# A decoder's wide cross-attention: where the key and query projections stand in TensorE's round

## The chip, the cores and the metric

The kernel runs on one core of a Trainium2 chip. The core has TensorE (matmuls), VectorE, ScalarE, GpSimd and SyncE, which work from queues of their own and wait for each other on semaphores. The metric is the device time of one execution in microseconds; the time of the kernel before is the median of three runs, 3679.55 us.

## The reference

Two decoder layers on x of 1024 x 128, each with self-attention, cross-attention to a context of 6404 x 96, and a small mixture of experts. The change lies in the last cross-attention, with 16 heads of 64:

```
q = query @ w_q                      # 1024 x 1024, from x of 1024 x 128
k, v = split(context @ w_kv)         # 6404 x 1024 each
scores = einsum('bhqd,bhkd->bhqk', q, k) * 64 ** -0.5
attn = softmax(scores)
out = einsum('bhqk,bhkd->bhqd', attn, v)
x = x + out @ w_out + b_out
```

Everything is computed in fp32 accuracy: q and k are each split into a rounded part (hi) and a rest (lo), and scores are hi x hi + hi x lo + lo x hi.

## The kernel before

`wide_heads_and_experts` (from line 1947) computes this attention. The heads are taken in 8 pairs, the 1024 queries in 2 halves of 512, which makes 16 units. A unit goes through the 6404 keys in 51 steps of 128 keys. Two steps make a round, so there are 408 rounds. The two heads of a pair stand side by side in the array.

In each round TensorE does, in the order in which its block is written (the loop behind line 2469):

- `score` of two steps (L2432): 12 matmuls, three products for each of two heads and two steps, into four PSUM banks. ScalarE takes exp of each step (L2595) into a ring of six buffers.
- `early`: one pair of maximum matmuls (L2387), bf16, two heads at once, for the *next* unit: they give rough scores from which VectorE takes the maximum of each row (L2668, two reductions), which is subtracted later ahead of exp.
- `weigh` of the two steps before (L2458): the value products, four pairs of fp32 matmuls that accumulate in bank 4.
- `whole`: at most one other piece of work (below).
- `late`: the remaining maximum pairs of the round, mostly one.

The pieces in `whole` are called items: "k" (L2405) projects 512 keys (the last chunk of 13 has 260) of the next pair of heads, "q" (L2398) projects the 512 queries of the unit after the next, "t" (L2393) turns the maxima, "s" (L2410) adds up the sums of the exponentials, and "y" (L2416) is the output projection. A planner at the head of the function hands them out: a "k" item in every sixth step (91 in the loop, 8 in an even unit and 5 in an odd one), one "q" item per unit until unit 13 (14), and one of each of the others per unit.

All items and the maximum pairs share a ring of three PSUM banks (`SIDE`, `BANKS` = 3). A maximum pair takes the next two banks, an item the next one; each waits (`wait_place`) until what stood in its bank three places earlier has been read. For a "k" item ScalarE first copies the result (L2556, `att_k_raw`), after the two exponentials of the round; then VectorE subtracts that copy from the result in PSUM (L2686, `att_k_step`), which frees the bank. In the next round ScalarE rounds (L2576, L2580), and in the one after that GpSimd makes the rest (L2264). For "q" ScalarE makes two copies (L2552, L2553) and VectorE subtracts (L2677). Each engine goes through the items in the order early, whole, late. VectorE's queue is therefore: reductions of the early pair, in some rounds a piece of a reciprocal (L2701), the subtraction of the item, reductions of the late pairs.

GpSimd adds the exponentials of half of the steps into a total (L2305) and issues DMAs that add the others (L2294). SyncE loads the values in groups of four steps.

Of the kernel before, what the change touches and what calls it, by code (L numbers as in the profile page):

```python
# [1946 lines left out]
def wide_heads_and_experts(nc, name, net_name, PS, ident, ctxT, xn, xnT, x, O, A, values, out, wide):  # L1947
# [61 lines left out]
    tiled, whole, taken, turned = [], [], PER_UNIT, 1  # L2009
    for j in range(STEPS):  # L2010
# [9 lines left out]
        items = whole[-1]  # L2020
# [11 lines left out]
            items.append(("k", p + 1, f))  # L2032
    last_items = [("s", UNITS - 1), ("y", UNITS - 1)]

    early = [items[:1] for items in tiled]
    late = [items[1:] for items in tiled]
    order = first + [item for items in zip(early, whole, late) for part in items for item in part] + last_items
# [13 lines left out]
    def top_later(item):  # L2051
        return item[1] > 0 and item[2] < KF - 1
# [78 lines left out]
    def bank_of(item, s=0):  # L2131
        return first_bank[item] + s if item in first_bank else SIDE + (place[item] + s) % BANKS
# [4 lines left out]
    def strip(s):  # L2137
        return slice(s * DH2, (s + 1) * DH2)

    def chunk(f):  # L2140
        return slice(f * HALF, min(NCTX, (f + 1) * HALF))
# [4 lines left out]
    with ExitStack() as stack:  # L2146
# [204 lines left out]
        def _(pe):  # L2351
            def wait_first(item):

                if item in copy_number:
                    pe.wait_ge(tile_copied, copy_number[item] + 1)
                elif item is not None:
                    pe.wait_ge(dve_freed, dve_count[item + (1,) if item[0] == "m" else item])

            def wait_place(at):
                if at < BANKS:  # L2360
                    wait_first(ring_user[at])
                else:
                    who, count = freed[at - BANKS]
                    pe.wait_ge(dve_freed if who == "dve" else negated, count)

            def side(item):
                kind, n = item[0], item[1]
                alone = item in first_bank
                if alone:
                    wait_first(first_user[item])  # L2370
                else:
                    wait_place(place[item])
                if kind == "m":
                    if not alone:
                        wait_place(place[item] + 1)
                    c, qt = item[2:]
                    p = n // HALVES
                    w = min(HALF, NCTX - c * HALF)
                    if qt == 0:
                        if c == 0:  # L2380
                            pe.wait_ge(kept, hi_count[("q", n)])
                        if n % HALVES == 0 and not top_later(("k", p, c)):
                            pe.wait_ge(kept, hi_count[("k", p, c)])
                        if n % HALVES == 0 and top_later(("k", p, c)):
                            pe.wait_ge(topped, top_number[("k", p, c)])
                    for s in range(2):
                        ins = pe.matmul(PS[:, bank_of(item, s), 0:w], q_top[strip(s), n % 2, qt * P:(qt + 1) * P],  # L2387
                                        k_top[strip(s), c * HALF:c * HALF + w], start=True, stop=True,
                                        tile_position=(s * DH2, 0))
                elif kind == "t":  # L2390
                    pe.wait_ge(top_ready, 2 * (n + 1))
                    for qt in range(QT):
                        ins = pe.transpose(PS[:, bank_of(item), qt * P:(qt + 1) * P], top[:, qt, :], ident[:, :])  # L2393
                elif kind == "q":
                    p, hf = n // HALVES, n % HALVES
                    if hf == 0:
                        pe.wait_ge(in_loaded[p % 2], 32 * (p // 2 + 1))
                    ins = pe.matmul(PS[:, bank_of(item), :], wq[:, p % 2, :], xnT[:, hf * HALF:(hf + 1) * HALF],  # L2398
                                    start=True, stop=True)
                elif kind == "k":  # L2400
                    p, f = n, item[2]
                    if f == 0:
                        pe.wait_ge(in_loaded[p % 2], 32 * (p // 2 + 1))
                    c = chunk(f)
                    ins = pe.matmul(PS[:, bank_of(item), 0:c.stop - c.start], wk[:, p % 2, :], ctxT[0:DC, c],  # L2405
                                    start=True, stop=True)
                elif kind == "s":
                    pe.wait_ge(folded, n + 1)
                    for s in range(2):
                        ins = pe.matmul(PS[strip(s), bank_of(item), :], ones_wide[:, :], total[:, n % 2, s, :],  # L2410
                                        start=True, stop=True, tile_position=(0, s * DH2))
                else:
                    pe.wait_ge(scaled, n + 1)
                    pe.wait_ge(out_loaded[n // HALVES % 2], 16 * (n // HALVES // 2 + 1))
                    for qt in range(QT):
                        ins = pe.matmul(PS[:, bank_of(item), qt * D:(qt + 1) * D], out_u[:, qt * P:(qt + 1) * P],  # L2416
                                        wo[:, n // HALVES % 2, :], start=True, stop=True)
                ins.then_inc(side_filled, 1)

            def score(j):  # L2420
                n, kt = j // KT, j % KT
                p, hf, b = n // HALVES, n % HALVES, 2 * (j % 2)
                if j >= 2:
                    pe.wait_ge(exped, j - 1)
                if kt == 0:
                    pe.wait_ge(dve_freed, dve_count[("q", n)])
                if kt % 4 == 0 and hf == 0:
                    pe.wait_ge(lo_left, lo_number[("k", p, kt // 4)])
                keys = slice(kt * P, (kt + 1) * P)
                for k, q, last in ((k_hi, q_hi, False), (k_hi, q_lo, False), (k_lo, q_hi, kt >= 2)):  # L2430
                    for s in range(2):
                        i = pe.matmul(PS[:, b + s, :], k[p % 2][strip(s), keys], q[n % QBUFS][strip(s), :],  # L2432
                                      start=kt < 2 and k is k_hi and q is q_hi, stop=last,
                                      tile_position=(s * DH2, 0), skip_group_check=kt >= 2)
                if kt >= 2:
                    i.then_inc(scored, 1)

            def subtract_maxima(j):

                n, kt, b = j // KT, j % KT, 2 * (j % 2)  # L2440
                if kt == 0:
                    pe.wait_ge(negated, negated_count[("t", n)])
                for s in range(2):
                    r = 32 * (b + s)
                    i = pe.matmul(PS[:, b + s, :], key_ones[r:r + 32, :], minus_max[r:r + 32, :],
                                  start=False, stop=True, tile_position=(r, 0))
                i.then_inc(scored, 1)
# [21 lines left out]
            for j in range(0, STEPS, 2):  # L2469
                score(j)  # L2470
                if j % KT == 1:
                    subtract_maxima(j)
                score(j + 1)
                if j % KT == 0:
                    subtract_maxima(j)
                if (j + 1) % KT < 2:
                    subtract_maxima(j + 1)
                for item in early[j // 2]:
                    side(item)
                between = j >= 2 and (j - 1) % KT == 0  # L2480
                if j >= 2:
                    weigh(j - 2)

                    if between:
                        assert not whole[j // 2]
                        for item in late[j // 2]:
                            side(item)
                    weigh(j - 1)
                for item in whole[j // 2] + ([] if between else late[j // 2]):
                    side(item)  # L2490
                if j // KT == LAST:
                    if j % KT == NET["turn"]:

                        pe.wait_ge(dve_freed, dve_count[("y", LAST - 1)])
                        pe.wait_ge(negated, negated_count[("s", LAST - 1)])
                        net.turn_tokens(pe, net.glue(0), 0)
                    if j % KT == NET["score"]:
                        net.score(pe, 0)
                    if j % KT == NET["turn_gates"]:
                        net.turn_gates(pe, 0)  # L2500
                    if j % KT == NET["spread"]:
                        net.spread_gates(pe, 0, 0)
# [560 lines left out]
```

## Time and profile before

| | |
|---|---|
| median of 3 runs | 3679.55 us (3679.04 to 3690.73) |
| the profiled execution | 3683.04 us |
| its span (first to last instruction) | 3681.3 us |
| TensorE matmuls busy | 3390.7 us, 92% |
| VectorE, ScalarE, GpSimd busy | 69%, 62%, 62% |
| first score of the wide attention | 1683.7 us after the span's start |

"Busy" is the time in which at least one instruction of an engine is under way. Matmuls overlap and their ends are modelled, so the distance from one start to the next says more than the duration of one. In a timeline, the time in brackets is the idle time of the engine just before the row, with what ended it. Rows with a count (x2, x4) are several instructions of one form merged, with the time from the first's start to the last's end.

### The profile page before, as it was taken

What the parts mean: (1) busy time and instruction counts of PE and PEld (TensorE: products, weight loads), DVE (VectorE), ACT (ScalarE), POOL (GpSimd) and SP (SyncE); (2) the same over time, 40 slices, a digit from 0 to 9 for tenths busy, and PEclk for the clock granted to TensorE, in tenths of its full rate; (3) what the DMA queues carried; (4) which work ended last, traced back from release to release, by engine and by line L of the source; (5) the groups of instructions that cost most, each with busy time, mean ns of one, the idle gap of its engine ahead of it and who ended that gap; (6) DMA issues with size and microseconds to landing.
All of it is one profiled execution on the core that took longest, in us unless ns stands there. A gap on an engine that the chain in (4) does not pass through costs nothing.

```text
span 3681.3 us, 58339 instructions
## 1 busy us (share of the span) xinstructions
PE 3390.7 (92%) x21696; PEld 1320.1 (36%) x21696; DVE 2537.5 (69%) x4290; ACT 2283.1 (62%) x2759; POOL 2268.9 (62%) x1564
## 2 busy tenths in 40 slices
PE   5877999999999989988999999999999999999999
PEld 2331222222222224433444444444444444444444
DVE  5748888888888835766666666666666666665842
ACT  4657888888888873575555555555555555555422
POOL 3124565665656600305888888888888888888800
PEclk7968999999999999978999999999999999999999
DMA  4111002002000100343566666676666766678100
GB/s 138 55 34 21 1 2 37 2 1 37 1 2 1 54 1 5 145 159 77 123 139 147 131 137 128 141 148 131 134 130 143 143 133 134 132 166 192 29 0 6
DMA packets 123729, 307.46 MB, mean 84 GB/s; under 512 B 15395, under 2 KB 31861, under 8 KB 122773
## 3 DMA queue, kind: packets, MB, share of 16 engines
q0 software_dynamic: 49680, 180.90, 24.7%
q1 hardware_dynamic: 73772, 122.82, 12.2%
q8 instruction: 179, 2.93, 0.3%
q14 instruction: 98, 0.80, 0.1%
HBM read 88.15 MB, written 34.64 MB: 33 GB/s over the span
## 4 chain that ended last, share of the span: by engine, by line
PE 47%; DVE 5%; ACT 2%; issue 1%; POOL 0%; DVEq 0%; ACTq 0%
PE PS L2458 20%; PE PS L2432 12%; PE PS L2387 6%; PE PS L2405 3%; DVE att_top_piece L2668 2%; PE PS L340 2%; PE PS L348 1%; DVE att_k_step L2686 1%; PE PS L341 1%; ACT att_k_raw L2556 1%; PE PS L2398 1%; PE PS L2416 0%; DVE k_xn L2725 0%; PE PS L2410 0%; ACT att_prob L2547 0%
## 5 line engine op out<-in xcount | busy, mean ns | idle before, releaser
L2668 DVE TENSOR_REDUCE att_top_piece<-PS 128x1 f32<-128x512 f32 (+1 forms) x1560 | 968.9, 665 | 346.0 <-PE PS L2387 343.4
L2305 POOL TENSOR_TENSOR att_total<-att_total,att_prob 128x1024 f32<-128x1024 f32 (+1 forms) x417 | 1053.5, 2526 | 152.2 <-ACT att_prob L2595 143.7
L2595 ACT ACTIVATE att_prob<-PS 128x1024 f32<-128x1024 f32 x816 | 792.6, 1021 | 562.7 <-PE PS L2432 501.3
L1781 ACT ACTIVATE att_prob<-PS 128x1024 f32<-128x1024 f32 (+2 forms) x912 | 892.3, 1004 | 178.5 <-PE PS L1623 175.7
L1878 DVE TENSOR_REDUCE att_top_piece<-PS 128x1 f32<-128x512 f32 (+1 forms) x1459 | 905.3, 665 | 131.9 <-PE PS L1591 126.7
L2458 PE MATMUL PS<-att_prob,att_vals 128*64 128x512 f32 x3264 | 794.5, 607 | 5.7 <-issue 4.9
L1646 PE MATMUL PS<-att_prob,cross_Vst 128*32 128x256 f32 (+1 forms) x5544 | 506.7, 431 | 2.1 <-issue 0.2
L1493 POOL TENSOR_TENSOR att_stage<-att_stage,att_run 128x512 f32<-128x512 f32 x150 | 191.1, 1274 | 401.6 <-ACT att_stage L1760 401.3
L1591 PE MATMUL PS<-cross_Kstack,cross_Qmax 49*128 49x512 bf16 (+1 forms) x1664 | 323.4, 386 | 95.5 <-DVE att_top_piece L1878 33.5
L2432 PE MATMUL PS<-att_q_hi,att_k_hi 64*128 64x512 f32 x1632 | 395.2, 480 | 4.2 <-POOL att_k_lo L2264 2.6
L2387 PE MATMUL PS<-att_k_top,att_q_top 64*128 64x512 bf16 (+1 forms) x1664 | 325.3, 389 | 76.1 <-DVE att_top_piece L2668 66.8
L2432 PE MATMUL PS<-att_q_hi,att_k_lo 64*128 64x512 f32 x1632 | 323.8, 393 | 0.0
L2432 PE MATMUL PS<-att_q_lo,att_k_hi 64*128 64x512 f32 x1632 | 322.3, 391 | 0.0
L1623 PE MATMUL PS<-cross_Qscore,cross_Kstack 49*128 49x512 bf16 x1632 | 308.6, 380 | 10.6 <-ACT att_prob L1781 6.3
L2458 PEld LDWEIGHTS PS<-att_prob,att_vals 128*64 128x64 f32 x3264 | 198.0, 136 | 332.1 <-issue 244.5
L1591 PEld LDWEIGHTS PS<-cross_Kstack,cross_Qmax 49*128 49x128 bf16 x1664 | 100.5, 93 | 490.0 <-DVE att_top_piece L1878 340.2
L2387 PEld LDWEIGHTS PS<-att_k_top,att_q_top 64*128 64x128 bf16 x1664 | 84.3, 93 | 510.3 <-DVE att_top_piece L2668 288.0
L1495 POOL TENSOR_SCALAR att_stage<-att_stage 128x512 f32<-128x512 f32 x150 | 222.8, 1486 | 13.1
L1646 PEld LDWEIGHTS PS<-att_prob,cross_Vst 128*32 128x32 f32 x5544 | 110.4, 108 | 275.5 <-ACT att_prob L1781 189.2
L1497 POOL TENSOR_TENSOR att_run<-att_run,att_stage 128x512 f32<-128x512 f32 x150 | 190.8, 1272 | 12.5
L2264 POOL TENSOR_TENSOR att_k_lo<-att_k_step,att_k_hi 128x512 fp32r<-128x512 f32 (+1 forms) x104 | 152.9, 1480 | 73.3 <-ACT att_k_hi L2580 73.1
L2686 DVE TENSOR_TENSOR att_k_step<-PS,att_k_raw 128x512 f32<-128x512 f32 (+2 forms) x104 | 67.6, 650 | 180.7 <-ACT att_k_raw L2556 163.8
(328 smaller groups left out, 3684.2 us busy)
## 6 DMA issues: line engine op xcount, KB each, us to landing
k_O<-att_prob POOLq DMA_DIRECT2D x180, 512.0 KB
k_xn<-att_prob POOLq DMA_DIRECT2D x165, 512.0 KB, 5.3
att_vals<-values SPq DMA_DIRECT2D x192, 256.0 KB, 3.0
values<-att_prob SPq DMA_DIRECT2D x14, 1024.0 KB, 4.1
values<-cross_Vall SPq DMA_DIRECT2D x10, 1024.0 KB, 4.2
cross_Kstack<-kparts SPq DMA_DIRECT2D x36, 204.0 KB
f_w<-in_f_w SPq DMA_DIRECT2D x24, 256.0 KB, 4.5
kparts<-cross_Vst SPq DMA_DIRECT2D x24, 128.0 KB, 1.8
```

Source lines behind the costliest of these rows:

```text
L1495: pool.tensor_scalar(now, now, 0.0, None, ALU.max).then_inc(tile_ahead, 1)
L1591: i = pe.matmul(PS[:, banks[item][s], 0:w], Qm[rows, g % 2, a, at:at + P], Kst[rows, g % 2, a, c * HALF:c * HALF + w], start=True, stop=Tr ...
L1623: i = pe.matmul(PS[:, 2 * (e % 2) + s, lo:HALF], Kst[rows, g % 2, a, kt * P:(kt + 1) * P], Qs[rows, g % 2, a, n % HALVES * HALF + lo:(n % ...
L1646: ins = pe.matmul(PS[r:r + 32, PV, lo:queries.stop], Vst[:, u % 2, kt, s, :], prob[:, j % RING, par, s, lo:queries.stop], start=(i == 0), ...
L1781: act.activation(prob[:, j % RING, par, :, lo:HALF], PS[:, 2 * (e % 2):2 * (e % 2) + 2, lo:HALF], ACT.Exp, scale=scale).then_inc(exped, 1)
L1878: dve.tensor_reduce(top_piece[:, n % 2, s * QT + qt, c:c + 1], PS[:, banks[item][s], 0:w], AX, ALU.max).then_inc(dve_freed, 1)
L2305: pool.tensor_tensor(so_far, so_far, prob[0:rows, j % RING, :, :], ALU.add).then_inc(summed, 1)
L2387: ins = pe.matmul(PS[:, bank_of(item, s), 0:w], q_top[strip(s), n % 2, qt * P:(qt + 1) * P], k_top[strip(s), c * HALF:c * HALF + w], start ...
L2432: i = pe.matmul(PS[:, b + s, :], k[p % 2][strip(s), keys], q[n % QBUFS][strip(s), :], start=kt < 2 and k is k_hi and q is q_hi, stop=last, ...
L2458: i = pe.matmul(PS[strip(s), PV, :], vals[:, value_slot(n, kt // 4), kt % 4, strip(s)], prob[:, j % RING, s, :], start=(kt == 0), stop=(kt ...
L2595: act.activation(prob[:, j % RING, :, :].rearrange("p a b -> p (a b)"), PSf[:, b:b + 2 * HALF], ACT.Exp, scale=scale).then_inc(exped, 1)
L2668: dve.tensor_reduce(top_piece[:, n % 2, s * QT + qt, c:c + 1], PS[:, bank_of(item, s), 0:w], AX, ALU.max).then_inc(dve_freed, 1)
```

## The change

In the planner each round's `whole` list is sorted so that "q" and "k" items come first. In TensorE's loop these items are issued between the early maximum pair and the value products; all other items stay behind the products. The blocks of the other engines are not touched.

```diff
@@ -2032,6 +2032,8 @@
             items.append(("k", p + 1, f))
     last_items = [("s", UNITS - 1), ("y", UNITS - 1)]
 
+    for items in whole:
+        items.sort(key=lambda item: item[0] not in ("q", "k"))
     early = [items[:1] for items in tiled]
     late = [items[1:] for items in tiled]
     order = first + [item for items in zip(early, whole, late) for part in items for item in part] + last_items
@@ -2478,6 +2480,9 @@
                 for item in early[j // 2]:
                     side(item)
                 between = j >= 2 and (j - 1) % KT == 0
+                projected = [item for item in whole[j // 2] if item[0] in ("q", "k")]
+                for item in projected:
+                    side(item)
                 if j >= 2:
                     weigh(j - 2)
 
@@ -2486,7 +2491,7 @@
                         for item in late[j // 2]:
                             side(item)
                     weigh(j - 1)
-                for item in whole[j // 2] + ([] if between else late[j // 2]):
+                for item in whole[j // 2][len(projected):] + ([] if between else late[j // 2]):
                     side(item)
                 if j // KT == LAST:
                     if j % KT == NET["turn"]:
```

## Rows read from the trace of the kernel before

**Rows 1.** The page, chain that ended last, share of the span by line.
```profile
PE PS L2458 20%; PE PS L2432 12%; PE PS L2387 6%; PE PS L2405 3%; DVE att_top_piece L2668 2%; PE PS L340 2%; PE PS L348 1%; DVE att_k_step L2686 1%; PE PS L341 1%; ACT att_k_raw L2556 1%; PE PS L2398 1%; PE PS L2416 0%; DVE k_xn L2725 0%; PE PS L2410 0%; ACT att_prob L2547 0%
```

**Rows 2.** Windows: stretch and length, then busy us of PE, PEld, DVE, ACT, POOL; clock.
```profile
2500.00:3290.00 790.00, 759.50 (x4504) 335.65 (x4502) 512.84 (x832) 431.78 (x515) 670.34 (x414) 1.00 0.66 138
```

**Rows 3.** Waits from 1800 to 3300: waiter, awaited, total us, times, longest.
```profile
POOL att_total L2305 <- ACT att_prob L2595: 110.1, 86, 2.8
...
PE PS L2387 <- DVE att_top_piece L2668: 56.0, 104, 1.2
```

**Rows 4.** Timeline of TensorE, a projection round and two plain rounds: start us, us, what.
```profile
2396.48 0.58 PE L2432 MATMUL PS<-att_q_hi,att_k_hi 64*128 64x512 f32 x2
...
2400.25 1.13 PE L2405 MATMUL PS<-k_ctxT,k_wk 96*128 96x512 f32 x2
2401.31 0.39 PE L2387 MATMUL PS<-att_k_top,att_q_top 64*128 64x512 bf16 x2
2401.35 0.58 PE L2432 MATMUL PS<-att_q_hi,att_k_hi 64*128 64x512 f32 x2
...
2403.48 0.39 PE L2387 MATMUL PS<-att_k_top,att_q_top 64*128 64x512 bf16 x2 [0.39 <-DVE att_top_piece L2668]
...
2405.71 0.58 PE L2432 MATMUL PS<-att_q_hi,att_k_hi 64*128 64x512 f32 x2
...
2407.06 0.40 PE L2432 MATMUL PS<-att_q_hi,att_k_lo 64*128 64x512 f32 x2
2407.30 0.39 PE L2387 MATMUL PS<-att_k_top,att_q_top 64*128 64x512 bf16 x2
2407.61 1.94 PE L2458 MATMUL PS<-att_prob,att_vals 128*64 128x512 f32 x8
2409.49 0.39 PE L2387 MATMUL PS<-att_k_top,att_q_top 64*128 64x512 bf16 x2
2409.52 0.58 PE L2432 MATMUL PS<-att_q_hi,att_k_hi 64*128 64x512 f32 x2
```

**Rows 5.** Timelines of VectorE and of ScalarE in the same rounds.
```profile
2402.05 0.69 DVE L2686 TENSOR_TENSOR att_k_step<-PS,att_k_raw 128x512 f32<-128x512 f32 x1 [2.26 <-ACT att_k_raw L2556]
2402.65 2.55 DVE L2668 TENSOR_REDUCE att_top_piece<-PS 128x1 f32<-128x512 f32 x4
...
2406.10 1.29 DVE L2668 TENSOR_REDUCE att_top_piece<-PS 128x1 f32<-128x512 f32 x2
2407.73 1.29 DVE L2668 TENSOR_REDUCE att_top_piece<-PS 128x1 f32<-128x512 f32 x2 [0.33 <-PE PS L2387]
...
2412.75 0.94 DVE L2701 RECIPROCAL att_sums<-att_sums 128x128 f32<-128x128 f32 x1
...
2401.42 0.60 ACT L2556 ACTIVATE att_k_raw<-PS 128x512 f32<-128x512 f32 x1 [1.90 <-PE PS L2405]
...
2406.80 1.94 ACT L2595 ACTIVATE att_prob<-PS 128x1024 f32<-128x1024 f32 x2 [1.24 <-PE PS L2432]
```

**Rows 6.** Timelines of TensorE, VectorE, ScalarE behind a query projection's round.
```profile
1966.86 0.58 PE L2432 MATMUL PS<-att_q_hi,att_k_hi 64*128 64x512 f32 x2
...
1972.77 0.58 PE L2432 MATMUL PS<-att_q_hi,att_k_hi 64*128 64x512 f32 x2
...
1968.05 0.69 DVE L2677 TENSOR_TENSOR att_q_lo<-PS,att_q_hi 128x512 fp32r<-128x512 f32 x1 [1.89 <-ACT att_q_top L2553]
...
1967.42 0.59 ACT L2553 ACTIVATE att_q_top<-PS 128x512 bf16<-128x512 f32 x1
```

**Rows 7.** Timeline of TensorE behind a short key projection's round.
```profile
2104.26 0.40 PE L2432 MATMUL PS<-att_q_hi,att_k_lo 64*128 64x512 f32 x2
2104.60 0.39 PE L2387 MATMUL PS<-att_k_top,att_q_top 64*128 64x512 bf16 x2
```

**Rows 8.** Timeline of TensorE, a projection round with two late pairs.
```profile
1704.44 0.58 PE L2432 MATMUL PS<-att_q_hi,att_k_hi 64*128 64x512 f32 x2
...
1711.44 0.39 PE L2387 MATMUL PS<-att_k_top,att_q_top 64*128 64x512 bf16 x2 [1.78 <-DVE att_top_piece L2668]
```

## The prediction

> **What bounds the kernel now.** I read the chain that ended last first: TensorE lines carry most of it, and VectorE's maximum (L2668) and key subtraction (L2686) appear in it for 2% and 1% of the span [rows 1]. So TensorE is the bound, and something on VectorE gets onto its path in places. The windows by stage come next: in a stretch of the wide attention, TensorE is busy 759.50 of 790.00 us at a granted clock of 1.00, which is its upper level, 2.4 GHz; VectorE has 512.84 and GpSimd 670.34 [rows 2]. At most 4% is there to win in this stage, if nobody works faster. The waits say where it is: in 1500 us TensorE waited 56.0 us for VectorE's maximum, 104 times, and GpSimd waited for the exponentials (110.1 us on one line alone), so it keeps up [rows 3]. The same list names only TensorE as what ScalarE's exponentials wait for, never GpSimd or a DMA.
>
> The timeline shows which rounds wait. Take the first score of a round as time 0. A plain round (2405.71 to 2409.52) lasts 3.81 us: early pair at 1.59, value products from 1.90, late pair at 3.78 [rows 4]. The round with a key projection (2396.48 to 2401.35) lasts 4.87; the projection stands at 3.77 and the late pair at 4.83 [rows 4]. The round behind it is as plain as the other, yet lasts 4.36 (2401.35 to 2405.71), because its early pair goes at 2.13 and not at 1.59 [rows 4]: 0.54 lost. Its cause can be read off the other engines. The projection comes out at the round's end, 1.17 us after its issue ScalarE copies it (2401.42, 0.60), VectorE, which has nothing else it may do, stands idle 2.26 us until that copy and subtracts (2402.05, 0.69), and only then reduces the late pair (from 2402.65) [rows 5]. In the plain round those reductions begin at 0.39 and end at 1.68 (2406.10 plus 1.29) [rows 5]; here they begin at 1.30. The early pair needs the bank of the first of them and goes 0.14 us after it ends.
>
> **The change part by part.** No instruction is added or taken away. The 91 key and 14 query projections of the loop (no round holds two) go ahead of the four value products, and the two products' waits, the exponentials of the previous round, are long met. The sort does nothing: each round of the planner's list holds at most one item of the kind it sorts. The order in which the results are counted (early, whole, late) and the ring of three banks stay as they were, so ScalarE, VectorE and GpSimd keep their order, and no queue of SP is passed. What moves is the start of each projection, from 3.77 to about 1.90, and of its round's products, from 1.90 to 2.96 (1.06 is the distance from projection to late pair, 2400.25 to 2401.31) [rows 4].
>
> New timetable of a projection round: early pair 1.59; projection 1.90; products 2.96; late pair 2.96 + 1.88 (2407.61 to 2409.49) = 4.84; end 4.87, as before [rows 4]. ScalarE ends its two exponentials at 3.03 (2406.80 plus 1.94) [rows 5] and the result is there at 1.90 + 1.17 = 3.07, so the copy runs to 3.67 and the subtraction from 3.70 to 4.39. VectorE has finished the early reductions at 3.31 (2407.73 plus 1.29); in rounds with a piece of the reciprocal (0.94) it is free at 4.25 and ends the subtraction at 4.94 [rows 5]. The late pair reaches VectorE only 0.43 us after its issue (2407.30 to 2407.73) [rows 4, 5], at 5.27. So the subtraction fits into a gap, the late reductions start at 0.40 of the next round, as in a plain one, and that round's early pair goes at 1.59. The stall behind a key projection goes whole; what is late next is TensorE's own stream, 3.81 us.
>
> A query projection has two copies and then its subtraction. Now the latter starts at 1968.05, 1.19 into the round (1966.86), and the round behind it, which holds a key projection too, lasts 5.91 (1966.86 to 1972.77) and not 4.87: 1.04 lost [rows 6]. Afterwards: the second copy ended at 1968.01 (1967.42 plus 0.59) [rows 6], 1.15 after the round's start, where a key's copy begins at 0.07 (2401.42) [rows 5], so about 1.08 for both; 3.07 + 1.08 = 4.15, subtraction to 4.87, or 4.94 behind a reciprocal, still ahead of 5.27. This stall goes as well.
>
> The waits the projection itself has: its bank is the third of the ring, last held by the second half of the previous round's late pair, whose reduction ends at 1.68 [rows 5]. With the 0.14 of a release that is 1.82, and TensorE comes there at 1.90: no wait, by 0.08 us. Behind a round with a reciprocal the reductions end at most 0.1 later. Queued behind this wait are now the products; nobody waits for these soon (the exponentials reuse their buffer six steps on, values are loaded three groups ahead).
>
> The trace has no projection between a maximum pair and a product, so its borders are priced from both sides. The pair of score matmuls takes 0.24 (2407.06 to 2407.30), the early pair before products 0.31: a border of about 0.08 [rows 4]. Products to late pair are 1.88, where four of 0.43 (1.94 us for all four with their tail) would be 1.72: 0.16. A new border may cost 0.16 more or less than the one it replaces: 105 x 0.16 = 17 us either way. I take 0, because a projection has two borders in either place and its cost between products and late pair, 1.06, already holds both kinds. The Trainium skill, "TensorEngine Tiling (Array Packing)", Key Properties, says that a change of the tiling mode drains TensorE. By that rule the sum stays: pair, projection, products, pair are three changes of mode, as are pair, products, projection, pair. No run here shows the drain apart.
>
> The sum. Of the 91 key projections 7 are short (260 columns). Behind a short one the early pair stands 0.34 behind the last score (2104.26 to 2104.60), against 0.24: 0.1 x 7 = 0.7 [rows 7]. Two of the 84 long ones stand in rounds with two late pairs. There the second late pair waits for reductions that are behind the subtraction: it goes at 7.00 (1704.44 to 1711.44) [rows 8]. Afterwards it goes at 5.27 + 0.65 + 0.14 = 6.06: 0.94 x 2 = 1.9. The other 82 are followed by a round that loses 0.55: 45.1. Queries: 14 x 1.04 = 14.6. Together 0.7 + 1.9 + 45.1 + 14.6 = 62.3 us. The profiled execution took 3683.0 (span 3681.3 and 1.7 around it), 3.5 above the median of the runs. From its time the sum gives 3620.7, from the median of 3679.6 it gives 3617.
>
> **The rivals.**
> A, the stall is given back in part: the margin of 0.08 us is not there, because the projection's bank is freed a little later or the release takes longer at this place, or the borders cost more. For: 0.08 is less than one release of 0.14. Against: the plain rounds repeat to 0.01 us, and a release that is due before TensorE arrives costs nothing. At 0.3 us for each of 105 projections 31 us come back: 3648.
> B, nothing: what is removed on TensorE is at once taken by the next, GpSimd. Its 670.34 us of 790 [rows 2] would have to fit into some 760: 88%. It waits for ScalarE now [rows 3], so I hold that for unlikely; in that case 3679.
> C, slower: the projection waits for reductions of its own round. Place: the wait for its bank, ahead of the products. If the bank were one of the early pair's, free at 3.31 + 0.14 = 3.45 [rows 5], TensorE would stand 1.55 us in each of 105 rounds: 163 - 62 = 101 more, 3780. It decides from a wait of 62.3 / 105 = 0.6 us, a bank free later than 2.4 instead of 1.68. Against: the ring's arithmetic (pair 2 banks, projection the third).
> D, the change doesn't do what it says: the subtraction is not what holds the early pair. Then the round lengths stay, 3679. Against: idle time and release agree in each of the rounds read [rows 4, 5, 6].
>
> **How the numbers follow.** The forecast, all stalls gone, with the border's bounds: 3617, 3600 to 3634, chance 0.76. A 0.13 (3634 to 3660), B and D 0.05 (3668 to 3690), C 0.06. The likeliest case gives 3617. For 8 in 10 I take the lower bound a little in, 3603, and reach into A up to 3648. About 0.3% (11 us) is what a measurement of this kernel can tell from no change; all of the forecast and of A lie beyond it: faster 0.89, same 0.05, slower 0.06.
>
> **What would show it.** In the profile afterwards: rounds with a projection stay at 4.87, the ones behind them fall to 3.81, a key round behind a query round from 5.91 to 4.87. TensorE's wait for L2668 ahead of L2387 falls from 56 us in 1500 to under 20, what is left standing at the units' beginnings. VectorE's idle time ahead of L2686 stays of the order of 0.4 us each. Wrong would be: a new wait at the projections (L2405, L2398) on L2668 (A, C), value products dearer behind a projection (A), exponentials waiting for GpSimd (B), or unchanged 4.36 us rounds (D).

## The result and the profile after

The changed kernel takes 3617.58 us (median of 4 runs, 3616.33 to 3618.99). The kernel before, with one more run on the same chip, has a median of 3682.96 us (3679.04 to 3690.73). The ratio is 0.9832, with a 95% interval of 0.9814 to 0.9849. The forecast was 3617, reckoned from the first three runs' median of 3679.6: 62 us less. Measured by the four runs, it is 65 us less.

The profiled execution spans 3617.3 us, 64.0 less than that of the kernel before. The window of the wide attention, to be laid beside [rows 2] (columns as there):

```profile
2500.00:3200.00 700.00, 691.68 (x4140) 307.63 (x4140) 477.95 (x765) 398.23 (x477) 616.92 (x381) 1.00 0.68 142
```

TensorE is busy for 98.8% of this stretch, not 96.1%, at the same granted clock, its upper level of 2.4 GHz. GpSimd is at 88%, as the text of rival B had worked out, and still waits for ScalarE. The list of waits from 1800 to 3300 us has these rows, beside [rows 3]:

```profile
POOL att_total L2307 <- ACT att_prob L2600: 82.2, 75, 1.8
...
DVE att_k_step L2691 <- ACT att_k_raw L2561: 23.3, 57, 0.5
PEld PS L2407 <- DVE att_top_piece L2673: 16.5, 70, 0.3
PE PS L2389 <- DVE att_top_piece L2673: 15.2, 15, 1.2
```

TensorE's wait ahead of the maximum pairs is down from 56.0 us in 104 places to 15.2 us in 15 places. Seven of these are at the start of an even unit, where the prediction expected what is left, but the other eight are at the end of one. VectorE's subtraction waits 0.4 us each time (23.3 / 57). The projection's weight loads name VectorE 70 times, but its matmuls have no such row: they start 0.32 us behind the early pair, except in one kind of round (below).

The same three rounds as in [rows 4], TensorE:

```profile
2366.36 0.58 PE L2434 MATMUL PS<-att_q_hi,att_k_hi 64*128 64x512 f32 x2
...
2367.94 0.39 PE L2389 MATMUL PS<-att_k_top,att_q_top 64*128 64x512 bf16 x2
2368.26 1.12 PE L2407 MATMUL PS<-k_ctxT,k_wk 96*128 96x512 f32 x2
2369.32 1.94 PE L2460 MATMUL PS<-att_prob,att_vals 128*64 128x512 f32 x8
2371.19 0.39 PE L2389 MATMUL PS<-att_k_top,att_q_top 64*128 64x512 bf16 x2
2371.23 0.58 PE L2434 MATMUL PS<-att_q_hi,att_k_hi 64*128 64x512 f32 x2
...
2372.81 0.39 PE L2389 MATMUL PS<-att_k_top,att_q_top 64*128 64x512 bf16 x2
...
2375.04 0.58 PE L2434 MATMUL PS<-att_q_hi,att_k_hi 64*128 64x512 f32 x2
```

The projection round lasts 4.87 us (2366.36 to 2371.23), as before. The round behind it lasts 3.81 (to 2375.04) and not 4.36, and its early pair goes at 1.58 and not at 2.13. VectorE and ScalarE in the same rounds, beside [rows 5]:

```profile
2368.38 1.29 DVE L2673 TENSOR_REDUCE att_top_piece<-PS 128x1 f32<-128x512 f32 x2 [0.34 <-PE PS L2389]
2370.06 0.69 DVE L2691 TENSOR_TENSOR att_k_step<-PS,att_k_raw 128x512 f32<-128x512 f32 x1 [0.39 <-ACT att_k_raw L2561]
2371.62 1.29 DVE L2673 TENSOR_REDUCE att_top_piece<-PS 128x1 f32<-128x512 f32 x2 [0.87 <-PE PS L2389]
...
2367.45 1.94 ACT L2600 ACTIVATE att_prob<-PS 128x1024 f32<-128x1024 f32 x2 [0.41 <-PE PS L2434]
2369.43 0.60 ACT L2561 ACTIVATE att_k_raw<-PS 128x512 f32<-128x512 f32 x1
```

The copy follows the exponentials without a gap. The subtraction runs from 3.70 to 4.39 of its round, and the late reductions start at 5.26 (2371.62), when their own matmuls come out. What names VectorE's idle time ahead of them is now TensorE: in these rounds the order on VectorE costs nothing any more.

### The profile page after: what moved, and what is told of

Same layout as the page of the kernel before. It is cut to its first block, busy times and chain, and to the rows that moved or that the text cites. A ratio compares the mean times of both kernels' runs of the same rounds, so it can differ in the third digit from the quotient of the medians.

```text
span 3617.3 us, 58339 instructions
## 1 busy us (share of the span) xinstructions
PE 3369.8 (93%) x21696; PEld 1316.2 (36%) x21696; DVE 2548.1 (70%) x4290; ACT 2283.4 (63%) x2759; POOL 2269.3 (63%) x1564
## 4 chain that ended last, share of the span: by engine, by line
PE 52%; DVE 2%; issue 1%; ACT 1%; POOL 0%; DVEq 0%; ACTq 0%
PE PS L2460 21%; PE PS L2434 16%; PE PS L2389 6%; PE PS L2407 3%; PE PS L340 2%; PE PS L348 2%; PE PS L341 1%; PE PS L2400 1%; PE PS L2418 0%; DVE att_top_piece L2673 0%; DVE k_xn L2730 0%; ACT att_prob L2552 0%; PE PS L2412 0%; PE PS L2447 0%; PE PS L2395 0%
## 5 line engine op out<-in xcount | busy, mean ns | idle before, releaser
L2307 POOL TENSOR_TENSOR att_total<-att_total,att_prob 128x1024 f32<-128x1024 f32 (+1 forms) x417 | 1070.5, 2567 | 116.7 <-ACT att_prob L2600 108.4
L2296 POOL DMA_DIRECT2D k_O<-att_prob x165 | 163.2, 989 | 51.2 <-ACT att_prob L2600 48.0
```

The source lines that it names most:

```text
L2307: pool.tensor_tensor(so_far, so_far, prob[0:rows, j % RING, :, :], ALU.add).then_inc(summed, 1)
```

## The experiments

The theory is that of the prediction: a projection's subtraction stands ahead of the late reductions in VectorE's queue, and it waits for ScalarE's copy of a result that comes at the round's end. The rivals are that the gain belongs to the round as a whole, that it is in proportion to how much earlier the projection goes, or that it comes from the projection's own bank. "Loop" below is the time from the first score of the first round to the first score of the last one: 1806.8 us in the kernel before, 1748.5 in the changed one.

**One kind of projection alone.**

```diff
-                projected = [item for item in whole[j // 2] if item[0] in ("q", "k")]
+                projected = [item for item in whole[j // 2] if item[0] == "k"]
```

> The change for the key projections alone; the 14 query projections stay behind the products. Theory (VectorE's queue: the subtraction waits for ScalarE's copy and holds up the late reductions, each stall of its own): the 1.04 us behind each query round stay, 14 x 1.04 = 14.6 us of the 62.3 are not won, so about 3632 us, rounds behind a key 3.81, rounds behind a query 4.85 (plain) and 5.91 (key). Rival (the gain comes from the round as a whole, for example products that start later): the query rounds make no difference of their own beyond their share of the count, 14 of 105, so 8 us: 3626.

Measured: 3631.44 us (3626.0 to 3635.82), ratio 0.9863 (0.9848 to 0.9878). And with `== "q"`:

> The change for the 14 query projections alone. Theory: 14.6 us are won, 3680 - 15 = 3665; rounds behind a key stay at 4.36, rounds behind a query fall to 3.81 and 4.87. Rival (share by count): 8 us, 3672.

Measured: 3663.38 us (3661.43 to 3670.6), ratio 0.9954 (0.9939 to 0.9969). Both medians are within 2 us of what the theory gives, and 5 and 9 us from the rival. For the first run that decides nothing, since its single times reach down to the rival's 3626. The rounds decide: in the second run those behind a query last 3.81 and 4.86 us, those behind a key 4.36. The 14 rounds behind a query are 14.6 us shorter in all than before. The whole loop is only 11.3 shorter (1795.5), because in three of its first six rounds, which the edit doesn't touch, the lower granted clock cost 3.3 us more than it did in the kernel before. In the first run there is one surprise. The key round behind a query round lasts 6.09 us and not 5.91:

```profile
2169.77 0.39 PE L2389 MATMUL PS<-att_k_top,att_q_top 64*128 64x512 bf16 x2 [0.88 <-DVE att_top_piece L2673]
2170.27 1.13 PE L2407 MATMUL PS<-k_ctxT,k_wk 96*128 96x512 f32 x2
```

The projection goes 0.50 behind the early pair and not 0.32. The previous round's late reductions were held up by the query's subtraction, so the projection's bank came free late, with the products queued behind it. This is the mechanism of rivals A and C, 0.18 us in 7 rounds. The query part of the change takes it away.

**How much later may it go.** The projection between the two steps' products:

```diff
-                for item in projected:
-                    side(item)
                 if j >= 2:
                     weigh(j - 2)
+                for item in projected:
+                    side(item)
+                if j >= 2:
```

> The projection between the two steps' value products, some 0.9 us later than in the change. Theory: issue 2.80, result 3.97, key copy to 4.57, subtraction to 5.29, late reductions from 5.29 in place of 5.27: nothing lost for keys. Queries: copies to 5.05, subtraction to 5.77, the first late reduction ends at 6.42 and the next early pair can go at 1.69 in place of 1.59: 0.1 x 14 = 1.4 us. So about 3619. Rival (the gain is in proportion to how much earlier the projection goes: 1.87 us earlier gave 62): 0.97 us earlier gives 32, 3648.

Measured: 3637.42 us (3632.69 to 3642.6), ratio 0.9881 (0.9864 to 0.9898), loop 1764.9. Neither number. As the theory says, the stall is gone: rounds behind a key last 3.81, and behind a query 3.84. But each projection round lasts 5.02 and not 4.87. TensorE:

```profile
2377.12 1.08 PE L2460 MATMUL PS<-att_prob,att_vals 128*64 128x512 f32 x4
2378.13 1.12 PE L2407 MATMUL PS<-k_ctxT,k_wk 96*128 96x512 f32 x2
2379.18 1.08 PE L2460 MATMUL PS<-att_prob,att_vals 128*64 128x512 f32 x4
2380.19 0.39 PE L2389 MATMUL PS<-att_k_top,att_q_top 64*128 64x512 bf16 x2
```

Half of the products takes 1.01 us (2377.12 to 2378.13 and 2379.18 to 2380.19), so two halves take 2.02, where the whole takes 1.87 (2369.32 to 2371.19 in the changed kernel). 0.15 x 105 = 15.8 us, and the loop is 16.4 longer than in the changed kernel. The expectation had left out that this place adds a border: the products are cut in two.

**The other way round.** The projection goes behind the late pair, on TensorE and on VectorE, later than in the kernel before. Two new helpers split a list: `projections` gives its "q" and "k" items, `others` the rest.

```diff
...
-    order = first + [item for items in zip(early, whole, late) for part in items for item in part] + last_items
+    order = first + [item for e, w, l in zip(early, whole, late) for item in e + others(w) + l + projections(w)
+                     ] + last_items
...
-                for item in whole[j // 2] + ([] if between else late[j // 2]):
+                for item in others(whole[j // 2]) + ([] if between else late[j // 2]) + projections(whole[j // 2]):
...
-                for item in whole[j // 2] + late[j // 2]:
+                for item in others(whole[j // 2]) + late[j // 2] + projections(whole[j // 2]):
```

> The other way round: on TensorE and on VectorE the projection goes behind the late maximum pair, so it comes out even later than before the change, but nothing stands behind its subtraction in that round. Theory (what costs is only that the late reductions stand behind the subtraction on VectorE): late reductions run at 4.21 to 5.50, the subtraction at 5.89 to 6.58, which is 1.02 to 1.71 of the next round, ahead of its early reductions at 2.02; the stalls go as with the change, about 3617 (3612 to 3622). Rival (the projection has to come out earlier, because its own bank or its copy is what the early pair waits for, or because the products must cover the copy): the early pair waits as before or longer, 3680 or more.

Measured: 3638.97 us (3634.68 to 3644.77), ratio 0.9885 (0.987 to 0.9901), loop 1766.7. The kernel is 1.1% faster than before although every projection comes out later, and the rival's 3680 is refuted: the early pair doesn't need an early projection. One thing this run can't tell. In the order early, whole, late the next early pair takes the projection's bank and that of the first late reduction; in the turned order it takes the late pair's banks alone. So the run removes a possible wait for the projection's own bank too. That this wait wasn't the one that counted is read from the kernel before: the subtraction ended at 2402.74 (2402.05 plus 0.69), 0.74 us ahead of the early pair at 2403.48, and the first late reduction at 2403.34 (2402.65 plus the 0.69 that one takes), 0.14 ahead [rows 4, 5].

VectorE in a projection round and behind it:

```profile
2379.72 1.29 DVE L2675 TENSOR_REDUCE att_top_piece<-PS 128x1 f32<-128x512 f32 x2 [0.34 <-PE PS L2394]
2381.91 1.29 DVE L2675 TENSOR_REDUCE att_top_piece<-PS 128x1 f32<-128x512 f32 x2 [0.90 <-PE PS L2394]
2383.59 0.69 DVE L2693 TENSOR_TENSOR att_k_step<-PS,att_k_raw 128x512 f32<-128x512 f32 x1 [0.39 <-ACT att_k_raw L2563]
2384.78 1.29 DVE L2675 TENSOR_REDUCE att_top_piece<-PS 128x1 f32<-128x512 f32 x2 [0.50 <-PE PS L2394]
```

The late reductions come first (2381.91) and the subtraction fits ahead of the next early ones. What was won less than expected is again a border:

```profile
2381.48 0.39 PE L2394 MATMUL PS<-att_k_top,att_q_top 64*128 64x512 bf16 x2
2381.80 1.13 PE L2412 MATMUL PS<-k_ctxT,k_wk 96*128 96x512 f32 x2
2382.86 0.51 PE L2439 MATMUL PS<-att_q_hi,att_k_hi 64*128 64x512 f32 x2
...
2386.54 0.39 PE L2394 MATMUL PS<-att_k_top,att_q_top 64*128 64x512 bf16 x2
```

From late pair to late pair, one round on, it is 5.06 us (2381.48 to 2386.54). Projection and plain round together last 8.87, against 8.68 in the changed kernel: 0.19 for each of 105 projections, 20 us, where the loop is 18.2 longer (1.4 of the difference is a round of the changed kernel that a fall of the clock lengthened, below). Late pair and scores, which otherwise follow each other without a border, are parted here.

**The copy twice.** ScalarE copies each key projection twice.

```diff
+        copied_once, copied_twice = m.sem("copied_once"), []
...
+                    copied_twice.append(item)
+                    act.activation(k_raw[n % 2][:, to], PS[:, bank_of(item), 0:to.stop - to.start], ACT.Copy
+                                   ).then_inc(copied_once, 1)
+                    act.wait_ge(copied_once, len(copied_twice))
                     raw = act.activation(k_raw[n % 2][:, to], PS[:, bank_of(item), 0:to.stop - to.start], ACT.Copy)
```

> The kernel before with the same second copy. Theory: each second copy behind the products lengthens the wait of the next early pair by its whole duration: 84 x 0.63 for long keys and 7 x 0.4 for short ones, 56 us, and up to 8 before the loop: 3736 to 3744; rounds behind a key 4.99. Rival (the stall has another cause, the copy is covered): 3680 to 3688.

In the kernel before: 3742.1 us (3739.47 to 3743.15), ratio 1.0175 (1.016 to 1.019), loop 1865.6, 58.8 longer. Rounds behind a key last 4.99. Of the 58.8, 54.2 us are in the rounds behind a key and the two key rounds with two late pairs. The rest lies almost all in three other rounds, in each of which the granted clock fell to its lower level (near 1713, 1775 and 1819 us).

> The changed kernel with ScalarE's copy of each key projection (L2556 of before) done twice, one after the other; the result is the same. Theory: the subtraction ends at 4.39 + 0.63 = 5.02, still ahead of the late pair at 5.27, so the 91 copies of the loop cost nothing. The 13 before the loop may cost up to 13 x 0.6 = 8: 3617 to 3625. Rival (the copy is still on the path of the round): 91 x 0.6 = 55 more, 3672.

In the changed kernel: 3625.89 us (3616.01 to 3633.49), ratio 0.9859 (0.9835 to 0.9883), loop 1748.7, that is 0.2 us longer. The same addition costs 54 us in one place and nothing in the other. The whole kernel is 9.5 us slower than the changed kernel in the runs beside it (3616.42, below). The expectation allowed 8 for the 13 copies ahead of the loop. How much of the 9.5 is theirs stays open, because what lies ahead of the loop differs by more than that from trace to trace ("Luck in the last figure", below). The subtraction in each, VectorE, first in the kernel before with the second copy, then in the changed one:

```profile
2430.41 0.69 DVE L2691 TENSOR_TENSOR att_k_step<-PS,att_k_raw 128x512 f32<-128x512 f32 x1 [2.89 <-ACT att_k_raw L2561]
2431.01 2.54 DVE L2673 TENSOR_REDUCE att_top_piece<-PS 128x1 f32<-128x512 f32 x4
```

```profile
2376.33 0.69 DVE L2696 TENSOR_TENSOR att_k_step<-PS,att_k_raw 128x512 f32<-128x512 f32 x1 [1.02 <-ACT att_k_raw L2566]
2377.27 1.29 DVE L2678 TENSOR_REDUCE att_top_piece<-PS 128x1 f32<-128x512 f32 x2 [0.25 <-PE PS L2390]
```

VectorE's idle time ahead of the subtraction grows by 0.63 in both (2.26 to 2.89, 0.39 to 1.02). In the second it comes out of the wait ahead of the late reductions, which still has 0.25 left.

**What the rest is made of.** The 15 waits left are in rounds with two late pairs (one round has three), whose second needs a bank that the first one's reduction frees. This run moves all but the last late pair of such rounds between the products:

```diff
+                split = j >= 2 and not between and len(late[j // 2]) > 1 and len(projected) == len(whole[j // 2])
...
+                    elif split:
+                        for item in late[j // 2][:-1]:
+                            side(item)
                     weigh(j - 1)
-                for item in whole[j // 2][len(projected):] + ([] if between else late[j // 2]):
+                for item in whole[j // 2][len(projected):] + ([] if between else late[j // 2][-1:] if split
+                                                              else late[j // 2]):
```

> The changed kernel, and in rounds with two or more late pairs all but the last go between the two steps' products. Those rounds last 5.09 to 6.14 where the stream would need some 0.25 more than a plain round. Theory: the second late pair waits for the first one's reduction, so pulling the first one forward by about 0.9 us wins up to 0.9 in each of some 12 such rounds (7 at the end of even units, 5 in the first unit); the 7 at the start of even units win nothing, because the copy of the output stands ahead of the reductions on VectorE. 5 to 10 us less than the changed kernel: 3607 to 3612. Rival (VectorE's total work in such rounds is the bound): no difference, 3617.

Measured: 3611.72 us (3609.6 to 3615.64), ratio 0.9823 (0.9808 to 0.9838). The changed kernel beside it, on the same chip:

> The changed kernel once more, beside the others on the same chip: 3617 us, and the loop from its first to its last round some 58 us shorter than before. What the part ahead of the loop takes, which the change does not touch, should then agree with the kernel before to within the few us that the moments of TensorE's clock changes differ by.

Measured: 3616.42 us (3614.22 to 3625.89), ratio 0.9839 (0.9824 to 0.9855), loop 1746.3. The two medians differ by 4.7 us and the intervals overlap, so the times alone leave the rival open; the split version's loop is 1742.6. The rounds at the end of even units fall from 5.59 to 4.80, as expected. Those at the start are not neutral, though. They rise from 5.88 to 6.35:

```profile
2342.22 0.39 PE L2389 MATMUL PS<-att_k_top,att_q_top 64*128 64x512 bf16 x2
2342.54 1.08 PE L2460 MATMUL PS<-att_prob,att_vals 128*64 128x512 f32 x4
2345.10 0.39 PE L2389 MATMUL PS<-att_k_top,att_q_top 64*128 64x512 bf16 x2 [1.48 <-DVE att_top_piece L2678]
```

```profile
2343.67 0.69 DVE L2717 COPY att_out_u<-PS 128x512 f32<-128x512 f32 x1 [1.06 <-PE PS L2460]
2344.27 1.95 DVE L2678 TENSOR_REDUCE att_top_piece<-PS 128x1 f32<-128x512 f32 x3
```

There the copy of the output (L2717 of this run) stands ahead of the late reductions on VectorE and waits for the unit's last product. With the pair between the products, that product ends later, and so do copy and reductions. The next run leaves these rounds alone (`split = j >= 2 and j % KT and ...`):

> As the run that split the late pairs, but not in the rounds at the start of an even unit, which its trace shows lengthened from 5.88 to 6.36 us; the others keep what they won there (5.60 to 4.80 at the end of the 7 even units, 0.6 to 0.8 in five rounds of the first unit). Theory: 7 x 0.48 = 3.4 us less than that run and about 9 less than the changed kernel: 3608 (3605 to 3612). Rival (what is won at a unit's end is given back at the start of the next, whatever stands there): no better than that run, 3612.

Measured: 3609.38 us (3603.84 to 3613.02), ratio 0.9806 (0.9786 to 0.9827), loop 1736.6.

> The changed kernel beside it on the same chip: 3617 us, ratio to before 0.983 to 0.984; no two theories are told apart, it is the measure for the other run of this call.

Measured: 3616.94 us (3612.57 to 3622.43), ratio 0.983 (0.981 to 0.985), loop 1748.2. The last version is 7.6 us ahead of the changed kernel by the medians, but the two intervals against the kernel before overlap. In the traces the gain is plain: the loop is 11.6 us shorter, 9.2 of them in the 12 rounds that the split touches and the rest where the clock falls differ. The rounds at the start of even units are back at 5.88 while those at their end stay at 4.80. It is the best version seen.

## Why the prediction was right

**The cause.** The step that mattered is that VectorE "has nothing else it may do": a queue in order, in which the subtraction stands ahead of the late reductions. Four kinds of experiment bear it out: the order on the queues is turned round and the stall goes, though every projection comes out later (projection behind the late pair, with the trace's reading of the banks); only the copy is lengthened and the stall grows by just that, or not at all; each kind of projection gives its own share; and half of the advance in time gives the whole of the stall.

**The timetable.** Projection 1.90, products 2.96, late pair 4.84, end 4.87, subtraction from 3.70 to 4.39, late reductions at 5.27: the trace has 1.90, 2.96, 4.83, 4.87, 3.70 to 4.39, 5.26. For the query the worst case was a subtraction behind a reciprocal that ends at 4.94; the trace has it at 4.87 (2172.09 plus 0.69, in a round that starts at 2167.91), ahead of the late reductions at 2173.16:

```profile
2171.12 0.94 DVE L2706 RECIPROCAL att_sums<-att_sums 128x128 f32<-128x128 f32 x1
2172.09 0.69 DVE L2682 TENSOR_TENSOR att_q_lo<-PS,att_q_hi 128x512 fp32r<-128x512 f32 x1
2173.16 1.29 DVE L2673 TENSOR_REDUCE att_top_piece<-PS 128x1 f32<-128x512 f32 x2 [0.38 <-PE PS L2389]
```

**The sum.** Term by term, from the lengths of the rounds in the two traces: behind short keys 0.7 (predicted 0.7), rounds with a key and two late pairs 1.8 (1.9), the 82 behind long keys 44.8 (45.1), of which 3.6 in the 7 that hold a "t" item and 41.2 in the other 75, and queries 14.6 (14.6). That is 61.9 of 62.3. The borders cost nothing, as taken: a key round is 4.87 in both.

**What the sum didn't have.** The loop itself is 58.3 us shorter and not 61.9. In the first two rounds, where the granted clock is still at its lower level in part, 1.5 us were lost, because the loop now begins 5.8 us earlier and the clock rose only later; another fall near 1803 us cost 1.4 in one round (5.66 to 7.01). Both lie in rounds that the change doesn't shorten. Windows of the changed kernel, with the clock in the last column but two:

```profile
1678.00:1694.00 16.00, 14.25 (x64) 7.09 (x66) 7.21 (x13) 6.03 (x8) 7.81 (x5) 0.62 0.09 34
1794.00:1814.00 20.00, 17.72 (x94) 7.24 (x92) 12.02 (x20) 7.03 (x8) 19.30 (x9) 0.91 0.20 60
```

The kernel before has 0.68 from 1684 to 1694 us and 1.00 from 1705 on. The six key rounds behind an output projection last 4.97 in place of 4.87, 0.6 in all. That is rival A, found in 6 rounds: the margin of 0.08 us is not there where the addition to x precedes the late reductions on VectorE:

```profile
2198.88 0.69 DVE L2700 TENSOR_TENSOR k_x<-k_x,PS 128x512 f32<-128x512 f32 x1 [1.66 <-PE PS L2418]
2199.49 2.04 DVE L2673 TENSOR_REDUCE att_top_piece<-PS 128x1 f32<-128x512 f32 x3
```

```profile
2200.40 0.39 PE L2389 MATMUL PS<-att_k_top,att_q_top 64*128 64x512 bf16 x2
2200.82 1.13 PE L2407 MATMUL PS<-k_ctxT,k_wk 96*128 96x512 f32 x2
```

The reductions start at 0.67 of the round (2198.82) and not at 0.40, and the projection goes 0.42 behind the early pair and not 0.32. The prediction had looked for late reductions behind a reciprocal only, and not behind the addition.

**Luck in the last figure.** Of the 64.0 us between the two profiled executions 5.8 lie ahead of the loop, where the kernels don't differ: the first score comes at 1677.9 and not at 1683.7. The two traces drift apart there mostly where the granted clock is at its lower level, in the first 220 us and near 1635 us. In the profiled executions of the other runs the loop begins between 1669.5 and 1687.0 us. So an agreement of the total to 1 us says little; an agreement of the loop to 4 us, and of nearly all its rounds to 0.01, says what the forecast was worth. By the same token the query share of 15 us and the last version's 9 us are read from the rounds. Against more runs of the kernel before, the changed kernel's saving by the medians is 62.1 us (7 runs of before) and 64.1 us (9 runs).

**Rivals.** B, C and D did not happen. GpSimd has 88% to do and keeps up; A's wait for the bank is 0.10 us in 6 rounds.

## What to carry to other kernels

Where an engine works its queue in order and one of its instructions waits for a second engine, count what stands behind that instruction. The transfer from TensorE over ScalarE to VectorE (here 1.17 + 0.60 + 0.69 us) has to be started so early that it ends before the next piece of the queue is due; starting it earlier than that brings nothing. Look for a place that keeps the number of changes of matmul shape: two other places removed the same stall and gave back some three tenths of the gain (16.4 and 18.2 of 58.3 us) at the array. And judge the change by the lengths of the rounds that it touches, because the rest of the program moves the total by several microseconds.

## What the runs showed of the hardware

The forecast's remark on borders turned out to be worth more than it was given. The Trainium skill, "TensorEngine Tiling (Array Packing)", Key Properties, has it that changing the tiling mode drains TensorE. The changed order has three changes in a round with a projection, as the old one; both orders of the experiments have four, and their projection rounds cost 0.15 us more (between the products) and 0.19 us more, taken over two rounds (behind the late pair). So the trace agrees with the rule, and the fourth change has a price here. That it is a drain, and not weights that can't be loaded ahead, no run tells apart.

Idle time in the trace is less than lost time: the early pair behind a projection shows 0.39 us of idle time [rows 4], but its round is 0.55 longer, since the modelled end of the last matmul covers the rest. A sum made of the waits would have come out some 30% too small.
